# A routed-expert loop on one Trainium2 core: rows loaded as 32-column pieces and transposed on VectorE instead of TensorE

## The reference, cut to what matters

```
h   = gelu(einsum('bsd,edf->ebsf', x, W1) + b1)      # 128 -> 512 per expert
y_e = einsum('ebsf,efd->ebsd', h, W2) + b2           # 512 -> 128
y   = einsum('ebsd,bse->bsd', y_e, P_norm)           # only 2 experts of 8 have weight
```

## Time and profile before

| | |
|---|---|
| median of three runs | 448.3 us |
| span of the profiled execution | 445.2 us |
| what lies around the span, by the median | 3.1 us |
| TensorE busy | 92% of the span, granted clock 0.997 on average |
| VectorE, ScalarE, GpSimd busy | 64%, 48%, 35% |
| DMA, mean | 92 GB/s, 64210 packets |

### The profile page before, as it was taken

The page is one execution under the profiler, slowest core; times in us unless marked ns, Lnnn a source line. Parts: engine busy times, 40 slices in busy tenths (PEclk is TensorE's granted clock), DMA queues, the critical chain, the costliest instruction groups (busy, mean ns, idle before and its releaser), DMA issues. The chain is left out here.

```text
span 445.2 us, 9851 instructions
## 1 busy us (share of the span) xinstructions
PE 409.0 (92%) x2944; PEld 344.6 (77%) x2944; DVE 284.5 (64%) x1137; ACT 213.8 (48%) x525; POOL 155.7 (35%) x215
## 2 busy tenths in 40 slices
PE   7699989999999999999988999888999999999882
PEld 7579777878869779787767779777899999998630
DVE  4889889888887878878867657412233343433327
ACT  3364555565554545543424353333555555555412
POOL 6340015013233340443433011534454555455510
PEclk9999999999999999999999999999999999999998
DMA  7449411154064330131222223321222222222576
GB/s 181 123 114 166 57 40 42 50 170 135 13 192 122 81 79 25 47 83 53 75 54 61 66 51 80 101 80 54 68 71 67 78 71 71 61 77 68 169 275 193
DMA packets 64210, 40.80 MB, mean 92 GB/s; under 512 B 18340, under 2 KB 57128, under 8 KB 64168
## 3 DMA queue, kind: packets, MB, share of 16 engines
q1 hardware_dynamic: 59472, 31.27, 28.2%
q0 software_dynamic: 4352, 8.99, 6.1%
q10 hardware_dynamic: 344, 0.03, 0.1%
HBM read 21.78 MB, written 18.48 MB: 90 GB/s over the span
## 5 line engine op out<-in xcount | busy, mean ns | idle before, releaser
L694 POOL DMA_INDIRECT routed<-send,slot x64 | 64.5, 1008 | 129.1 <-DMA routed<-send,slot 57.5
L703 POOL DMA_INDIRECT results<-nat,y_to x72 | 69.8, 969 | 89.0 <-DVE nat L1638 65.4
L1029 PE MATMUL psA<-xuT,w_all 128*128 128x256 f32 x288 | 68.9, 381 | 3.5 <-ACT h1T L1239 3.2
L1239 ACT ACTIVATE h1T<-psA,b1T 128x256 f32<-128x256 f32 x144 | 63.1, 473 | 12.0 <-PE psB L1052 7.5
L1029 PEld LDWEIGHTS psA<-xuT,w_all 128*128 128x128 f32 x288 | 50.6, 190 | 11.5 <-issue 2.9
L1041 PE MATMUL psC<-w_all,h1T 128*128 128x128 f32 x464 | 56.7, 275 | 1.0 <-DVE nat L1622 1.0
L1610 DVE TENSOR_SCALAR xu<-ring 128x256 f32 (+1 forms) x38 | 11.2, 295 | 71.2 <-DMA ring<-routed 67.0
L1041 PEld LDWEIGHTS psC<-w_all,h1T 128*128 128x128 f32 x464 | 54.1, 192 | 1.3 <-ACT h1T L1239 1.1
L1230 ACT ACTIVATE xuT<-psB 128x256 f32<-128x256 f32 x37 | 14.2, 383 | 61.6 <-PE psB L1019 45.8
L843 PE MATMUL psB<-xnT,w_l 128*128 128x512 f32 x64 | 34.3, 618 | 0.0
L1170 ACT ACTIVATE hg0T<-psB,b1T 128x512 f32<-128x512 f32 x32 | 22.0, 688 | 22.9 <-PE psB L845 22.8
(11 more groups left out here) (289 smaller groups left out, 851.8 us busy)
## 6 DMA issues: line engine op xcount, KB each, us to landing
ring<-routed SPq DMA_DIRECT2D x38, 130.0 KB
inv<-inv_room SPq DMA_DIRECT2D x8, 512.0 KB
w_all<-results SPq DMA_DIRECT2D x15, 256.0 KB, 4.1
routed<-ring SPq DMA_DIRECT2D x24, 130.0 KB, 6.7
n_room<-nT SPq DMA_DIRECT2D x8, 256.0 KB
w_all<-in_L_ffn_W_dram SPq DMA_DIRECT2D x1, 2048.0 KB
out_dram<-x_all SPq DMA_DIRECT2D x8, 256.0 KB, 2.3
results<-nat,y_to POOLq DMA_INDIRECT x72
```

The source lines that it names most:

```text
L694: pool.indirect_dma_start(routed[:, :], bass.IndirectOffsetOnAxis(ap=slot[par][:, c, t:t + 1], axis=0), send[par][:, c, t, :], None).then_ ...
L703: pool.indirect_dma_start(results[:, :], bass.IndirectOffsetOnAxis(ap=y_to[:, par, a:a + 1], axis=0), yw[:, par, a, :], None).then_inc(S[f ...
L1029: last = mm(psA[:, j // 2, (j % 2) * UNIT:(j % 2 + 1) * UNIT], w1_all[:, e, j * P:(j + 1) * P], xuT[:, :], start=True, stop=True)
L1239: f(h1T[:, j, :], psA[:, j // 2, (j % 2) * UNIT:(j % 2 + 1) * UNIT], ACT.Gelu, bias=b1T[:, n:n + 1]).then_inc(S["gelu_ready"], 1)
```

## The change

Each unit's 128 value columns come as four pieces of 32 columns, so that piece c fills partitions 32c to 32c+31 with eight blocks of 32x32 side by side; id and weight come as a fifth DMA into a ring of their own with eight slots. Each of the five has its own semaphore and waits for its own previous landing. The four slots of `ring` are freed by `take` (`xu_ready`) and no longer by `results_of`. VectorE copies a slot to `xu` as before and then turns all blocks with one 32x32 block transpose of 128x256, `turn`, which writes `xuT`. TensorE's two transposes and ScalarE's copy go. VectorE's `take_ahead(u)` now waits until `hid(u)` is through, turns u+1, and takes u+2.

```diff
+TO_RING = 8
+BLOCK = 32
+PIECES = P // BLOCK
+UNIT_IN = tuple(f"piece{c}_in" for c in range(PIECES)) + ("to_in",)
...
+        ring_x = ring.rearrange("p r a d -> p r (a d)")[:, :, 0:UNIT]
+        ring_iw = sb("ring_iw", [P, TO_RING, HALVES, 2])
...
             def load_unit(u, row):
-                wait_on(sp, "unit_in", u * 16)
+                if not isinstance(u, int) or u >= RING:
+                    wait_on(sp, "xu_ready", u - RING + 1)
+                at = bass.ds(u % RING, 1)
+                rows = routed[bass.ds(row, UNIT), :]
+                for c in range(PIECES):
+                    sp.sem_inc(apart, 1)
+                    wait_on(sp, f"piece{c}_in", u * 16)
+                    sp.dma_start(ring_x[c * BLOCK:(c + 1) * BLOCK, at, :]
+                                 .rearrange("p r (b e) -> p (r b) e", e=BLOCK),
+                                 rows[:, c * BLOCK:(c + 1) * BLOCK]
+                                 .rearrange("(b p) e -> p b e", p=BLOCK)).then_inc(S[f"piece{c}_in"], 16)
                 sp.sem_inc(apart, 1)
-                wait_on(sp, "ring_free", u - RING + 1)
-                sp.dma_start(ring[:, bass.ds(u % RING, 1), :, :].rearrange("p r a d -> p (r a) d"),
-                             routed[bass.ds(row, UNIT), :].rearrange("(a p) d -> p a d", p=P)
-                             ).then_inc(S["unit_in"], 16)
+                wait_on(sp, "to_in", u * 16)
+                sp.sem_inc(apart, 1)
+                wait_on(sp, "ring_free", u - TO_RING + 1)
+                sp.dma_start(ring_iw[:, bass.ds(u % TO_RING, 1), :, :].rearrange("p r a w -> p (r a) w"),
+                             rows[:, COL_ID:].rearrange("(a p) w -> p a w", p=P)
+                             ).then_inc(S["to_in"], 16)
...
-            def turn(u):
-
-                pe.wait_ge(S["xu_ready"], u + 1)
-                for a in range(HALVES):
-                    last = tr(psB[:, 0, col(a)], xu[:, a, :], ident[:, :])
-                last.then_inc(S["xuT_ps"], 1)
...
-                turn(u + 1)
...
-            def turned(u):
-                act.wait_ge(S["xuT_ps"], u + 1)
-                f(xuT[:, :], psB[:, 0, 0:UNIT], ACT.Copy).then_inc(S["xuT_ready"], 1)
...
             def take(u):
 
-                wait_on(dve, "unit_in", u * 16 + 16)
-                v.tensor_scalar(xu[:, :, :],
-                                ring[:, bass.ds(u % RING, 1), :, 0:D].rearrange("p r a d -> p (r a) d"),
+                for c in range(PIECES):
+                    wait_on(dve, f"piece{c}_in", (u + 1) * 16)
+                    dve.sem_inc(apart, 1)
+                if not (isinstance(u, int) and u == 0):
+                    dve.wait_ge(S["xuT_ready"], u)
+                v.tensor_scalar(xu[:, :].unsqueeze(1), ring_x[:, bass.ds(u % RING, 1), :],
                                 1.0, None, ALU.mult).then_inc(S["xu_ready"], 1)
 
+            def turn(u):
+
+                wait_on(dve, "xu_ready", u + 1)
+                v.transpose(xuT[:, :], xu[:, :]).then_inc(S["xuT_ready"], 1)
+
             def take_ahead(u):
-                dve.wait_ge(S["xuT_ps"], u + 2)
+                dve.wait_ge(S["hid_ps"], (u + 1) * (JF // 2))
+                dve.sem_inc(apart, 1)
+                turn(u + 1)
                 take(u + 2)
...
                 wait_on(dve, "y_landed", u - 1)
-                at = ring[:, bass.ds(u % RING, 1), :, :]
+                dve.sem_inc(apart, 1)
+                wait_on(dve, "to_in", (u + 1) * 16)
+                at = ring_iw[:, bass.ds(u % TO_RING, 1), :, :]
```

More of the change, by code:

```diff
@@ L294, in two_block_kernel @@
         ring = sb("ring", [P, RING, HALVES, ROW])
-        xu = sb("xu", [P, HALVES, D])
+        ring_x = ring.rearrange("p r a d -> p r (a d)")[:, :, 0:UNIT]
+        ring_iw = sb("ring_iw", [P, TO_RING, HALVES, 2])
+        xu = sb("xu", [P, UNIT])
         xuT = sb("xuT", [P, UNIT])
@@ L375, in two_block_kernel @@
             "s1_ready",
-            "unit_in",
+            *UNIT_IN,
             "ring_free",
-            "xu_ready", "xuT_ps", "xuT_ready",
+            "xu_ready", "xuT_ready",
             "hid_ps",
@@ L388, in two_block_kernel @@
         )}
-        SEEDED = {"yb_ready": 1, "y_landed": 2, "unit_in": 1, "ring_free": RING, "h1_free": JF,
+        SEEDED = {"yb_ready": 1, "y_landed": 2, **{name: 1 for name in UNIT_IN}, "ring_free": TO_RING, "xu_ready": RING, "h1_free": JF,
                   "gelu_ready": JF, "yw_ready": 1}
@@ L482, in _ @@
                                  ring[:, n + 1 if n else e % 2, :, :]).then_inc(prefilled, 16)
-            sp.sem_inc(S["unit_in"], SEEDED["unit_in"])
+            for name in UNIT_IN:
+                sp.sem_inc(S[name], SEEDED[name])
             def load_unit(u, row):
-                wait_on(sp, "unit_in", u * 16)
-                sp.sem_inc(apart, 1)
-                wait_on(sp, "ring_free", u - RING + 1)
-                sp.dma_start(ring[:, bass.ds(u % RING, 1), :, :].rearrange("p r a d -> p (r a) d"),
-                             routed[bass.ds(row, UNIT), :].rearrange("(a p) d -> p a d", p=P)
-                             ).then_inc(S["unit_in"], 16)
+                if not isinstance(u, int) or u >= RING:
[9 more added lines that the diff above has]
+                                 .rearrange("(b p) e -> p b e", p=BLOCK)).then_inc(S[f"piece{c}_in"], 16)
+                sp.sem_inc(apart, 1)
+                wait_on(sp, "to_in", u * 16)
[4 more added lines that the diff above has]
+                             ).then_inc(S["to_in"], 16)
             def work(step, g):
@@ L563, in _ @@
             load_unit(bounds[E] + 1, 0)
-            wait_on(sp, "unit_in", (bounds[E] + 2) * 16)
-            sp.sem_inc(apart, 1)
+            for name in UNIT_IN:
+                wait_on(sp, name, (bounds[E] + 2) * 16)
+                sp.sem_inc(apart, 1)
             def load_results(c, to, signal):
@@ L1064, in unit_work @@
                     wait_on(pe, "rank_read", groups - 1)
-                    turn(0)
+                    pe.sem_inc(apart, 1)
                 elif what == "hid":
@@ L1085, in _ @@
                     wait_on(pe, "s1_ready", groups)
-                elif g == 4:
-                    pe.wait_ge(S["xuT_ready"], bounds[E] + 1)
                 elif g == 6:
@@ L1246, in unit_work @@
             def unit_work(what, k=0):
[L1247 to L1251, removed]
+                if what == "gelu":
                     gelus(0, 0)
@@ L1259, in _ @@
             first_pass(act, work, unit_work)
-            other_units(act, bounds, lambda u, e: turned(u + 1), out)
+            other_units(act, bounds, lambda u, e: None, out)
             f(silu_first[:, :], b1T[:, 0:1], ACT.Silu)
@@ L1297, in weight_products @@
                 dve.sem_inc(S["ring_free"], SEEDED["ring_free"])
+                dve.sem_inc(S["xu_ready"], SEEDED["xu_ready"])
                 dve.sem_inc(S["yw_ready"], SEEDED["yw_ready"])
@@ L1626, in results_of @@
                 wait_on(dve, "y_landed", u - 1)
[L1627 removed]
+                dve.sem_inc(apart, 1)
+                wait_on(dve, "to_in", (u + 1) * 16)
+                at = ring_iw[:, bass.ds(u % TO_RING, 1), :, :]
                 mine = bass.ds(u % 2, 1)
                 v.tensor_scalar(y_to[:, mine, :].rearrange("p r a -> p (r a)").unsqueeze(2),
[L1630 removed]
+                                at[:, :, :, 0:1].bitcast(I32)
                                 .rearrange("p r a d -> p (r a) d"), 0.0, None, ALU.add)
[L1632 removed]
+                v.tensor_scalar(y_wt[:, :].unsqueeze(2), at[:, :, :, 1:2]
                                 .rearrange("p r a d -> p (r a) d"), 1.0, None,
@@ L1644, in unit_work @@
                     take(0)
-                    dve.wait_ge(S["xuT_ps"], 1)
+                    turn(0)
                     take(1)
```

## The result

The changed kernel takes **461.87 us** in the median (460.14 to 462.56), the kernel before, beside it on the same chip, 448.0 (446.05 to 448.49): a ratio of 1.0318, 95% interval 1.0284 to 1.0353. It is slower, as forecast, and 1.9 us from the predicted 460. The profiled execution has 462.56 us and a span of 460.8, so 1.8 us lie around the span.

What follows compares the result with a forecast made beforehand. TensorE bounded the kernel before; after the change SyncE's queue of five issues would, at T = 4.1 us a unit. 338.1 + 29 T gives 457.0, plus 3.1 us between span and median: 460 us, range 446 to 476.

Steps and rivals of the forecast that it cites:

- T: Loop over units: time SyncE's queue needs per unit, claimed 4.1 us against 3.73 before; break-even at 3.69.
- Turnaround: SyncE's queue in the loop: from a unit's last DMA to the head of the next, 0.62 us.
- Issues: SyncE's queue in the loop: five DMA issues of 0.382 us and four gaps, 2.09 us a unit.
- The 3.51 us without transposes: TensorE in the loop: a unit of 3.73 us loses 0.22 us of transposes, leaving 3.51.
- ScalarE's copy: ScalarE: removing a copy of 0.38 us a unit is worth nothing, as it has 38 us idle in 90.
- The first pass: Units ahead of the loop: SyncE's longer loads and TensorE's saving of 1.8 us set against each other, zero within 2 us.
- The entry: Start of the loop: SyncE's first issue at 305.78, the fourth piece at 307.7, its data used at 310.0.
- The end: After the loop: 28.1 us from the landing of the last unused load to the end of the kernel.
- A: Rival, the loop: SyncE keeps up and TensorE sets the pace, -6.2 us, 442 us; chance 0.13.
- B: Rival, SyncE's queue: nothing shared between pieces, each issue near 0.5 us, 4.9 us a unit, 483 us; chance 0.09.
- C: Rival, the transfers: small packets are the bound, 5.4 us a unit at twice the packet price, 498 us; chance 0.03.
- D: Rival, whole kernel: no difference, the loop's unit within 0.03 of 3.69 us; chance 0.03.

Runs made afterwards that it cites:

- e4: The changed kernel without four of SyncE's six event instructions a unit; 453.79 us, ratio 1.0188 to the kernel before.
- e5: The changed kernel with the loop's id and weight DMA issued by ScalarE and no longer by SyncE; 446.95 us, ratio 0.9998 to the kernel before.
- e1: The changed kernel without the fourth piece, so SyncE issues four DMAs a unit; 444.18 us, ratio 0.9958 to the kernel before.
- e12: e7 with SyncE's eight loads of the lower results issued ahead of its final waits; 447.15 us, ratio 1.0006 to the kernel before.
- e8: e5 with VectorE's copy of unit u+2 moved from the front of unit u-1's results to behind them; 449.69 us.
- e11: The kernel before the change, with only VectorE's copy moved behind the results; 450.99 us, ratio 1.0141 to the unedited kernel before.
- e6: The changed kernel without the two unused loads behind the last unit; 459.09 us, ratio 1.0265 to the kernel before.
- e2: The changed kernel with each piece loading only the first 128 of 256 rows, same five issues; 458.92 us, ratio 1.0302 to the kernel before.
- e10: e7 with VectorE's copy moved behind the results; 447.63 us, ratio 1.0047 to the kernel before.
- e7: The changed kernel with the edits of e5 and e6 and three event instructions fewer a unit on SyncE; 446.95 us, ratio 1.0009.
- e9: The changed kernel, all five issues kept on SyncE, with VectorE's copy moved behind the results; 458.76 us, ratio 1.0304 to the kernel before.

## Why the prediction was right

**The mechanism.** The step that decided, five issues in one queue, stands: spaced evenly, SyncE waiting for almost nothing, pace down to TensorE's as soon as one issue leaves. One issue alone is small, 0.33 us beside the 2.3 us of the earlier trace rows; taken as nothing for five in series it would have given 3.51 us a unit, and the trace has 4.03.

Three of the signs that the prediction named did not come. The last scatter started at 438.3 and not near 435 (see the end, below). VectorE's wait for pieces did not grow (45.4 us, before 51.4). And TensorE counts as busy for 91% of 320 to 410 us, not 86%; but matmuls overlap in these records, and by the starts it is 3.51 of 4.14 us, 85%.

**The terms of T.** Predicted 4.1; measured 4.03 in the even stretch, 4.09 from the data of unit 8 to the last unused load ((429.51 - 310.96) / 29). Turnaround 0.62 and 0.62. Events 0.40; by e4's 0.062 each, 0.37. Issues 2.09; measured 4 x 0.326 + 0.404 and four gaps, 1.87. I had kept 0.382 for the pieces, but the form with 32 partitions takes 0.326, near the 0.321 that the earlier trace rows had for it alone. What is left of 4.03, behind 0.16 for wait values, is 1.01 for addresses, where I had 0.81. So two errors of 0.2 cancelled, which is luck; the sharing of arithmetic that I assumed does occur (0.070 and 0.029 for most pieces), but the load of id and weight needs 0.110 and 0.029 again.

**TensorE.** The 3.51 us without transposes: 3.52 and 3.53 in e5, e1 and e12.

**VectorE.** The transpose takes 0.445 (taken 0.446) and is hidden: in e5 0.95 us lie between its end and the hidden layer. That nothing depends on the order there was an unspoken part of this step; e8 and e11 show that it holds for this order alone.

**ScalarE's copy** worth nothing: nothing here contradicts it; no run took it alone.

**The first pass**, zero within 2 us. Loads began at 247.95, 1.5 us later than in the trace before, ahead of any unit; a stretch at half clock (0.50 from 21.0 to 24.4 us) lies there, which the profiled execution before did not have. SyncE entered the loop at 306.13, against 303.68. So about 1 us of it may be the change.

**The entry:** data of unit 8 at 310.96, predicted 310.0. But I carried forward only SyncE's chain. What the late copy does to the sum of unit 5 behind it, and so to TensorE (idle 3.35 us), was not in my steps. It did no harm to the forecast, since SyncE's chain set the pace from there on. In e5 it took at most half of the 4.07 us that unit 8 is late; the rest is the late data itself, which VectorE copies at 310.64 there and at 306.97 in the kernel before (in e8, with the order changed, unit 8 is still 2.1 us behind).

**The end** was the term that was mis-sized: 28.1 us from the last unused load's data, measured 460.8 - 429.51 = 31.3. I took the intervals of before one by one. The step with the 2.2 us of the earlier trace rows was too short. These are GpSimd's two issues; but it gives its word only when the scatters of the unit before have landed, and those of unit 33, issued by 430.33, landed at 435.9, 5.6 us after the second issue, beside the lower results. From the first scatter of unit 34 to the last unit's id 4.4 us went by (432.11 to 436.48). From the last scatter on I had 21.7 and measured 22.5. That part holds a stretch at half clock (0.50 from 444.2 to 447.6), which the trace before has not; from the upper loads to the end the kernel after, e1, e6 and e12, with such a stretch just behind those loads, take 19.0 to 19.5 us, the kernel before and e2 to e5, e8, e10 and e11, without it, 17.9 to 18.1 (e7 and e9, where one ends ahead of them or as they start, 18.5 and 19.2). Of the 3.8 us by which the span exceeds the predicted 457.0, 3.2 are this term and 0.6 lie ahead of it; 1.8 us around the span in place of 3.1 give 1.3 back, and the median is 0.7 under the profiled execution.

**The rivals.** A (SyncE keeps up, 442): no; its condition is met only where SyncE has four issues, and there the time is 444 to 450, so its gain of 6.2 us was too high for the whole kernel. B (a dear queue): no, 0.326 an issue. C (packets): no, by e2; and a packet took less than the 34 ns of before, 0.322 x 460.8 x 16 / 100816 = 24 ns, at 1280 packets a unit. D: no.

## What to carry to other kernels

Count what an issuing queue spends on each DMA, its addresses, its wait value and its events, and compare the sum with the bound engine's time per unit before one transfer is cut into several; here a piece costs 0.60 us of the queue, and with half its packets (e2) its issue took the same 0.326 us. A transfer or copy that is hidden in the steady loop can still stand on the path at the loop's entry and end, so a gain per unit must be followed to the last instruction. And before a waiting operation is moved back in an engine's order, look who depends on what it feeds: in two kernels here (e8, e11) the move cost more than it freed, and in two (e9, e10) nothing could be told.

## What the runs showed of the hardware that was not expected

- A small transfer was late by several us beside 2 MB that another engine issued: a scatter was seen landed 5.5 us after its issue in e7, with 2 MB issued just ahead of it, and 2.3 us after it in e12, where the last of the 2 MB had been issued 7.4 us ahead. In e12, 2 KB of ids issued at 413.13 let VectorE go on only at 419.53, 6.40 us later.
- The granted clock fell to half (0.50 of full speed) for 3.4 us in stretches that the profiled execution before did not show: in e5 at 311.4, in the kernel after at 311.1 (with 3.35 us of idle TensorE ahead of it) and 444.2. In the window 300 to 320 of the kernel after the mean was 0.91. A group of matmuls that takes 1.95 us took 3.40. At the entry ten of the traces with pieces have such a stretch, with TensorE idle for 1.84 (e4) to 3.90 us (e3) ahead of it; e2 with 1.76 us and e10 with 3.32 us of idle time have none. So what brings it is not settled here by the idle time alone.
- An issue's duration on SyncE depends on its form: 0.326 us for a piece with 32 partitions, 0.404 for id and weight with 128, 0.382 for the former whole unit.
